# Latent attention: one sum over a diagonal key tile, after GpSimd has added its two halves of probabilities

## What is computed

```python
latent_kv = (x @ Wk + x @ Wv) @ W_down_kv
qh, kh, vh = heads(x @ Wq), heads(latent_kv @ W_up_k), heads(latent_kv @ W_up_v)   # 16 heads of 16
scores = clip(qh @ kh.T / 16, -1e4, 1e4)
scores = scores * exp(-1e-4 * abs(i - j))     # i a query's place, j a key's
out = softmax(scores) @ vh
```

## Time and profile before

| | |
|---|---|
| three runs | 1527.18, 1527.94, 1528.04 us; median 1527.94 |
| profiled execution | 1525.91 us, its span 1523.8 us |
| PE busy, of the span | 1253.3 us, 82% |
| DVE | 839.7 us, 55% |
| ACT | 758.3 us, 50% |
| POOL | 276.8 us, 18% |
| attention steps, 118 to 524 us | PE busy 397.9 of 406 us, POOL 95.7 |

### The profile page before, as it was taken

How to read it: one execution, slowest core, us unless ns; L and a number is a source line. 1 busy time by engine, 2 the same in 40 slices (tenths; PEclk the granted TensorE clock), 3 DMA queues, 4 the chain that set the end, 5 groups by cost and what they waited for, 6 DMA issues and landing times. The chain is left out here.

```text
span 1523.8 us, 26079 instructions
## 1 busy us (share of the span) xinstructions
PE 1253.3 (82%) x8850; PEld 751.7 (49%) x8851; DVE 839.7 (55%) x1883; ACT 758.3 (50%) x1473; POOL 276.8 (18%) x490
## 2 busy tenths in 40 slices
PE   4779999999999789881756998788864399999991
PEld 2214444444443364450234643644562299999991
DVE  5987777777776073347987445633345123233323
ACT  3817777777777624634844676235420133333330
POOL 2912222222222101120000000311204311111110
PEclk9859999999999998995568999889975599999996
DMA  6860451323030020000001000240044211111115
GB/s 206 266 176 23 116 146 46 84 65 84 24 85 3 1 92 1 2 4 17 1 1 33 2 1 0 69 194 2 5 138 146 67 36 35 38 35 38 35 35 173
DMA packets 66881, 96.09 MB, mean 63 GB/s; under 512 B 11090, under 2 KB 56948, under 8 KB 65236
## 3 DMA queue, kind: packets, MB, share of 16 engines
q1 hardware_dynamic: 61254, 83.29, 18.8%
q0 software_dynamic: 3408, 9.34, 1.7%
q10 hardware_dynamic: 2112, 2.10, 0.4%
HBM read 65.15 MB, written 29.17 MB: 62 GB/s over the span
## 5 line engine op out<-in xcount | busy, mean ns | idle before, releaser
L824 DVE CUSTOM_DVE_ANT_0 faded_scores_sb<-banks,inner_sb 128x1024 f32<-128x1024 f32 x256 | 303.4, 1222 | 92.4 <-PE banks L663 91.2
L923 ACT ACTIVATE xt_sb<-banks 128x512 f32<-128x512 f32 x344 | 179.0, 603 | 72.5 <-PE banks L670 72.4
L670 PE MATMUL banks<-q_stack_sb,k_stack_sb 99*128 99x128 bf16 (+3 forms) x960 | 180.9, 297 | 5.9 <-ACT xt_sb L923 2.6
L663 PE MATMUL banks<-k_stack_sb,q_stack_sb 96*128 96x512 bf16 (+3 forms) x704 | 163.6, 338 | 6.9 <-DVE peak_sb L824 3.8
L670 PEld LDWEIGHTS banks<-q_stack_sb,k_stack_sb 99*128 99x128 bf16 x960 | 70.5, 97 | 159.7 <-ACT xt_sb L923 66.7
L2083 PEld LDWEIGHTS banks<-slots_xt_sb,tile_w_sb 128*128 128x128 f32 x1248 | 146.9, 194 | 1.9
L2083 PE MATMUL banks<-slots_xt_sb,tile_w_sb 128*128 128x128 f32 x1248 | 147.0, 277 | 0.0
L2095 PE MATMUL banks<-experts_w_sb,xt_sb 128*128 x624 | 141.2, 379 | 1.3 <-issue 1.3
L2095 PEld LDWEIGHTS banks<-experts_w_sb,xt_sb 128*128 128x128 f32 x624 | 115.5, 190 | 15.8 <-issue 1.7
L2129 ACT ACTIVATE slots_xt_sb<-banks 128x256 f32<-128x256 f32 x39 | 15.0, 384 | 213.2 <-PE banks L2069 213.2
L923 ACT ACTIVATE probs_sb<-banks 128x512 f32<-128x512 f32 x168 | 87.4, 603 | 33.9 <-PE banks L670 33.9
(11 more groups left out here) (302 smaller groups left out, 2077.8 us busy)
## 6 DMA issues: line engine op xcount, KB each, us to landing
experts_w_sb<-in_L_ffn_W SPq DMA_DIRECT2D x16, 1024.0 KB, 12.0
k_stack_sb<-k_parts SPq DMA_DIRECT2D x48, 256.0 KB, 4.8
q_stack_sb<-q_parts SPq DMA_DIRECT2D x96, 128.0 KB, 3.5
q_parts<-parts_sb SPq DMA_DIRECT2D x16, 384.0 KB, 2.5
k_parts<-parts_sb SPq DMA_DIRECT2D x16, 384.0 KB, 3.7
slots_x<-zeros_sb SPq DMA_DIRECT2D x3, 1677.0 KB, 11.3
slots_x_sb<-slots_x SPq DMA_DIRECT2D x39, 129.0 KB, 2.1
xt_sb<-outputs_y SPq DMA_DIRECT2D x8, 512.0 KB, 6.3
```

The costliest lines, as they stand in the source:

```text
L663: last = pe.matmul(k.ps[:, 2 * (tile % 2) + half, lo - half * G:hi - half * G], stacks.q[0:ROWS, g % 3, version, h, j * P:(j + 1) * P], st ...
L670: return pe.matmul(k.ps[:, bank, at:at + hi - lo], stacks.k[0:ROWS + PARTS, g // 2 % 2, version, h, kt * P:(kt + 1) * P], stacks.q[0:ROWS ...
L824: dve.tensor_tensor_reduce(out=junk[:, tile % 2, :], in0=tile_scores(tile), in1=inner[:, window(tile)], scale=1.0, scalar=-3.0e38, op0=ALU ...
L923: act.activation(out, k.ps[:, bank_of((exp_done, u + 1)), :], ACT.Exp).then_inc(exp_done, 1)
```

## The change

POOL no longer leaves two masked halves. After the two selects it waits for both and adds `probs_d` onto the diagonal tile of `probs_of(s)` (in place, 128 partitions by 4 heads of 128 queries, float32) and raises a new semaphore, `joined`. PE waits for `joined` where it waited for `selected`, and leaves out the four matmuls over `probs_d`. ACT may overwrite a buffer of `probs_d` once the add that read it is done, where it waited for PE's sum before. The sum of a non-diagonal step, the masks and the exponentials stay as they are.

```diff
+    joined = k.sem("joined")
...
                 if on_diagonal(i):
-                    pe.wait_ge(selected, s // 2 + 1)
-                    lo = block_of(g, i) * P
-                    for h in range(HEADS):
-                        pe.matmul(k.ps[VW * h:VW * (h + 1), PV_BANK, lo:lo + P], vh[:, n % 2, h, kt, :],
-                                  probs_d[:, s // 2 % 2, h, :], start=False, stop=False, skip_group_check=True)
+                    pe.wait_ge(joined, s // 2 + 1)
...
                 pool.wait_ge(exp_done, unit_index(g, i, HEADS - 1) + 1)
-                pool.affine_select(later, later, [[0, HEADS], [1, P]], ALU.is_ge, 0.0, base=0, channel_multiplier=-1)
+                pool.affine_select(later, later, [[0, HEADS], [1, P]], ALU.is_ge, 0.0, base=0,
+                                   channel_multiplier=-1).then_inc(selected, 1)
                 earlier = probs_d[:, s // 2 % 2, :, :]
                 pool.wait_ge(exp_done, unit_index(g, i, HEADS) + 1)
                 pool.affine_select(earlier, earlier, [[0, HEADS], [-1, P]], ALU.is_gt, 0.0, base=0,
                                    channel_multiplier=1).then_inc(selected, 1)
+                pool.wait_ge(selected, 2 * (s // 2) + 2)
+                pool.tensor_tensor(later, later, earlier, ALU.add).then_inc(joined, 1)
...
-                    wait(act, summed, s - 3)
+                    wait(act, joined, s // 2 - 1)
```

## The result

Fourteen runs of each kernel, side by side: before 1525.64 us (1523.76 to 1528.04), changed 1532.14 us (1528.11 to 1534.51), ratio 1.0040 with a 95% interval of 1.0031 to 1.0049. That is 6 us slower, where +6.3 was forecast. The profiled execution's span went from 1523.8 to 1529.5 us.

What follows compares the result with a forecast made beforehand. PE was taken to bound the latent attention stage. Net stalls minus savings gave +2.4 (14 groups), +1.2 and +2.7 us (last two), +6.3 in all: 1527.9 + 6.3 = 1534.2 us, range 1526.5 to 1543.

Steps and rivals of the forecast that it cites:

- The saving of 0.22 us a sum: At PE's 64 diagonal sums, four matmuls over 128 queries go: 0.22 us each, 14.1 us in all.
- the step that failed: Behind PE's shortened diagonal sum, work is released by PE, so nothing else gives back the saving of 14.1 us.
- The 1.17 us: POOL's add of 512 elements estimated from the documented rate: path 2.00 us, total about +1.5 us, 1529.4.
- The path: From the start of POOL's second select to PE's load: select 0.63, wait 0.08, add 1.27, signal 0.12; 2.10 us.
- The stalls: PE's waits for POOL's add at i = 1, 3, 5, 7 of a full group: 0.52, 0, 0.10, 0.34 us.
- stalls that shrink because PE has another wait ahead of them: Sign of a wrong forecast, at PE's diagonal sums: another PE wait in the same place no longer occurs; no size given.
- The last two groups: Groups 14 and 15, where PE reaches the sums sooner: they cost +1.2 and +2.7 us.
- the add of 1.15 us: Rival at POOL's add: it takes the lower bound, so saving and stalls break even, about 1528 us; chance 0.20 with surroundings.
- DVE didn't hold it up: Rival at POOL's add: DVE holds it up to 1.49 to 1.60 us, +17 to +24 us, 1545 to 1552; chance 0.14.
- The hidden add: Rival at POOL's add: no longer than 0.75 us, so full groups have no stalls and time is 1516 us; chance 0.06.
- (1): Break-even rival at POOL's add: 1.15 us, total about 0, 1528 us; chance 0.20 with its surroundings.
- (3): Faster rival at POOL's add: no longer than 0.75 us, PE keeps its saving, 1516 us; chance 0.06.

Runs made afterwards that it cites:

- the one with the wait alone: Changed kernel, but POOL adds into a spare tile and PE waits for it yet keeps its four short matmuls; 1546.3 us, ratio 1.0146 to the kernel before.
- the kernel with sums and turn later: Changed kernel with every sum and the turning of the peaks one step later, which also moved POOL's split a step later; 1525.4 us, ratio 1.0002 to before.

## Why the prediction was right

- What bounds the stage: right. But for the second wait below, a microsecond of PE counts one for one; the kernel without an add, and the one with the wait alone, show it from either side.
- The saving of 0.22 us a sum: right where nothing else is late (0.887 for four with later sums), 0.82 for four in the old order. The statement that nothing gives it back was wrong by 0.06 us a group, 0.8 us in all: the step that failed took PE's chain to be released by PE alone, and overlooked that `turn_peaks` waits for DVE and POOL over the shortened sum.
- The add: 1.27 us taken, 1.267 measured, a median. The line through the rows of 256 and 32 elements held; the nearest row of the same length, with a bf16 operand, would have been 0.12 us off, and its median 0.33. The 1.17 us, an estimate from the rate in the Trainium skill, "GPSIMD Engine Reference", section 3.1, were 0.1 too short, so the measurement decides. (With 1.17 the prediction's own terms give about +1 us and not its +1.5.) The page's advice to put such an add on VectorE is not tested here; what the runs show is that the engine was no obstacle once the sum was asked for later.
- POOL's wait on itself, 0.08 us taken; 299.57 + 0.63 to 300.29 is 0.09 in the rounded rows. POOL to PE: 0.12 taken, 301.67 - 301.56 = 0.11. The path: 2.10 us forecast, 2.09 to 2.10 in three of four intervals.
- The stalls: 0.52, 0, 0.10 and 0.34 us forecast. At i = 5 it was about 0.05, since the second wait delays PE itself: with later sums, where the path is no limit, its interval is 2.05 us and not 2.00. This error and that of the saving are one cause with opposite signs, and nearly cancel: +0.17 forecast and +0.18 measured a group. That they cancel is luck, since the prediction saw neither. It did name, among the signs of being wrong, stalls that shrink because PE has another wait ahead of them, and the one at i = 5 is such a case.
- The last two groups: +3.9 us forecast. The last two distances between ACT's copies, which cover them, grew from 24.70 to 25.94 and from 22.17 to 24.96, by 1.2 and 2.8 us where 1.2 and 2.7 were forecast.
- The absolute forecast, 1534.2 us, is 2.1 over the median of 1532.1, because the three runs that it started from had a median 2.3 us over that of the fourteen. What was predicted well is the difference.
- Rivals: the add of 1.15 us did not come. DVE didn't hold it up: 58 of the 64 adds ran beside an operation of line 824 for a part of their time, and took 1.262 to 1.276 us; the six that met none took 1.260 to 1.268. So the row beside the DVE operation on PSUM was the one to go by. The hidden add was not reached; the run with half an add lies just below its threshold and agrees. The price between (1) and (3) was wrong, by the prediction's own terms: from about 0 at 1.15 us to -12 at 0.75 it is some 3 us for every 0.1 us of the add, and 5 only from 1.27 down to 1.15.

## What to carry to other kernels

A result that is handed over between engines has a length of path and a time at which it is asked for, and only their difference costs. It is read in a trace as an interval between two starts, at every place where the pair occurs: here 2.39 us was enough, 2.00 and less were not. The mean of the four, 1.93, would have priced the stalls of a group at 0.68 us where the single ones give 0.96. When work is moved from the bound engine to an idle one, first move the asking: one step more between the select and the sum turned 6 us of loss into some 19 us of gain against the kernel before, part of it from a wait that had nothing to do with the add. And when one engine gets faster, look for the next wait on its line that is fed from before the shortened part.

## What the hardware showed beyond the expected

- A POOL add of two float32 operands of 512 elements per partition takes 1.267 us (1.26 to 1.28) and of 256 elements 0.724, in place and with strided blocks of 128. The same add into a contiguous spare tile took 1.267 to 1.270 at the median, and an add of 256 elements elsewhere in the kernel 0.727.
- Where PE stood still before a sum, its first matmul began 0.03 us behind its weight load (301.67 and 301.70); from the first matmul to that of the next block it is 1.00 us in all sums of the changed kernel but the last, waited for or not. That is the 0.03 the prediction added for each stall.
- In the changed kernel the granted clock stayed at 1.00, the 2.4 GHz level, through all full groups, where PE stands still for up to 0.5 us in three of eight steps, and through the last groups with waits of 0.9 us. Before the very last sum PE waited 2.31 us; the clock fell to 0.50 at 528.8, within that sum, and the turn of the output behind it took 1.11 us where it took 0.66 before the change. Before the change PE's wait at that sum was 0.97, and the clock was 1.00 up to 524 us. With 1.3 us of standstill in each full group, in the kernel with sums and turn later, it was 1.00 up to 494 us and fell behind the wait of 1.91 shown above.
